# A transformer block with self and cross attention on one core: wider transfers, later weight splits, and another order at the seam to the feed-forward part

## What is computed

```
h = layernorm(x, ln1);  x = attention(h, h) + x          # 16 heads of 64
h = layernorm(x, ln2);  x = attention(h, context) + x
h = layernorm(x, ln3);  a, gate = split(h @ ff_w1 + ff_b1)   # 2 x 1024
x = (a * gelu(gate)) @ ff_w2 + ff_b2 + x
```

## Time and profile before

| | |
|---|---|
| median of 3 runs | 1717.55 us (1717.55 to 1719.23) |
| the profiled execution | 1720.14 us, its span 1718.3 us |
| PE busy | 1702.5 us (99%) |
| VectorE, ScalarE, GpSimd busy | 85%, 69%, 63% |
| moved by DMA | 263.99 MB, mean 154 GB/s |
| mean granted clock of PE | 0.999 |

### The profile page before, as it was taken

How to read it: one execution, slowest core, us unless ns; L and a number is a source line. 1 busy time by engine, 2 the same in 40 slices (tenths; PEclk the granted TensorE clock), 3 DMA queues, 4 the chain that set the end, 5 groups by cost and what they waited for, 6 DMA issues and landing times.

```text
span 1718.3 us, 42977 instructions
## 1 busy us (share of the span) xinstructions
PE 1702.5 (99%) x13628; PEld 1663.1 (97%) x13628; DVE 1467.4 (85%) x3184; ACT 1186.3 (69%) x3245; POOL 1087.9 (63%) x1812
## 2 busy tenths in 40 slices
PE   8999999999999999999999999999999999999999
PEld 8999999999999999999999999999999998888888
DVE  7888988888888888889999999999999997666665
ACT  6777777777777777777778878777777775222222
POOL 6777777766666666687778877777777665122211
PEclk9999999999999999999999999999999999999999
DMA  7777777676656666677777787776666662212110
GB/s 208 186 184 179 185 183 178 171 179 164 155 152 153 153 154 167 158 172 186 186 188 192 193 192 179 184 180 168 167 167 168 163 172 55 74 50 64 66 44 25
DMA packets 286641, 263.99 MB, mean 154 GB/s; under 512 B 102225, under 2 KB 246737, under 8 KB 286417
## 3 DMA queue, kind: packets, MB, share of 16 engines
q1 hardware_dynamic: 232624, 248.12, 57.1%
q10 hardware_dynamic: 53792, 13.12, 3.7%
HBM read 70.40 MB, written 24.90 MB: 55 GB/s over the span
## 4 chain that ended last, share of the span: by engine, by line
PE 90%; DVE 2%; SPq 2%; DMA 2%; POOL 2%; issue 1%; ACT 1%; ACTq 0%; POOLq 0%; DVEq 0%
PE QKB L341 19%; PE PVB L400 13%; PE PTB L355 12%; PE WOP L380 10%; PE VB L316 9%; PE S L303 6%; PE S L302 6%; PE PTB L920 5%; PE S L920 5%; PE QKB L936 3%; PE VB L936 3%; DMA RX<-QKS 1%; SPq L433 1%; SPq L435 1%; ACT PT L507 0%
## 5 line engine op out<-in xcount | busy, mean ns | idle before, releaser
L507 ACT ACTIVATE PT<-S,NM 128x256 f32<-128x256 f32 x1024 | 472.1, 474 | 186.0 <-DVE NM L613 185.6
L595 DVE TENSOR_TENSOR PL<-PTB,PH 128x512 fp32r<-128x512 f32 x512 | 349.4, 683 | 81.5 <-ACT PH L526 77.4
L811 POOL TENSOR_TENSOR ON<-ON,RB 128x256 f32<-128x256 f32 x256 | 188.9, 738 | 278.4 <-DVE ON L633 264.7
L613 DVE TENSOR_REDUCE NM<-S 128x2 f32<-128x512 f32 x512 | 325.9, 677 | 0.0
L526 ACT ACTIVATE PH<-PTB 128x1024 fp32r<-128x1024 f32 x256 | 263.4, 1029 | 90.3 <-PE PTB L355 87.3
L355 PE MATMUL PTB<-IDN,PT 128*128 128x128 f32 x2048 | 266.1, 273 | 0.1
L302 PE MATMUL S<-RX 128*128 128x256 f32 x1012 | 253.9, 283 | 0.2
L303 PE MATMUL S<-RX 128*128 128x256 f32 x1012 | 253.7, 283 | 0.0
L355 PEld LDWEIGHTS PTB<-IDN,PT 128*128 128x128 f32 x2048 | 229.5, 140 | 1.2 <-DVE PL L595 1.1
L380 PE MATMUL WOP<-WO,OT 128*128 128x256 f32 x1536 | 226.3, 283 | 2.3 <-POOL OT L816 2.3
L633 DVE TENSOR_TENSOR ON<-PVB,ON 64x256 f32<-64x256 f32 x512 | 213.1, 416 | 3.5
(11 more groups left out here) (142 smaller groups left out, 3142.4 us busy)
## 6 DMA issues: line engine op xcount, KB each, us to landing
RX<-QKS SPq DMA_DIRECT2D x506, 192.0 KB, 2.9
RX<-QKS SPq DMA_DIRECT2D x506, 128.0 KB, 2.8
RB<-denominators SPq DMA_DIRECT2D x512, 64.0 KB, 2.6
out_dram<-XR SPq DMA_DIRECT2D x32, 256.0 KB, 2.8
rows<-XN SPq DMA_DIRECT2D x24, 256.0 KB, 2.5
rows<-HF SPq DMA_DIRECT2D x23, 256.0 KB, 2.3
XR<-in_x_dram SPq DMA_DIRECT2D x16, 256.0 KB, 3.1
denominators<-RDT SPq DMA_DIRECT2D x256, 16.0 KB
```

Source lines behind the costliest of these rows:

```text
L507: last = e.activation(PT[:, c % 2, j * S:(j + 1) * S], S1[:, i, qt * S:(qt + 1) * S], ACT.Exp, bias=NM[:, j:j + 1], accum_out=DEN[:, c % 2 ...
L595: e.tensor_tensor(PL[:, cols], PTB[:, i, :], PH[:, s % 2, cols].bitcast(F32), ALU.subtract).then_inc(a.dve_pl, 1)
L613: e.tensor_reduce(NM[:, i * TT:(i + 1) * TT], S1[:, i, :].rearrange("p (t s) -> p t s", t=TT), AX.X, ALU.max, negate=True).then_inc(a.dve_ ...
```

## The change

1. `spread_den`: one transfer to all 128 partitions in place of two to 64 each. The source has the dimensions 2 (heads), 64 (the same row again, step 0) and 256. The counts on d_rb fall from 32 to 16 for each spread.
2. `stage`, `stage_rows`: one transfer for a staged matrix in place of two, except for the last 64 rows of the matrices with 192 rows; `staged(load)` gives the new counts.
3. `pool_weights`: the second halves of both output matrices are split one slot later (c = 5 to 8 and 131 to 134).
4. Chunk 0 is normalised in four slots, from ATT - 12 on, one tile of 256 columns each; the store of its second half moves from ATT - 9 to ATT - 8.
5. At slot ATT ScalarE does a Gelu on one column ahead of its first real one, after a wait for the transposes of slot ATT - 2; the first real Gelu waits for these too, not for the last ones, and the second waits for the small one (s_tab).
6. GpSimd makes RSTD of chunk 1 before its slot ATT + 2, not after that slot and the bias additions of chunk 0.
7. VectorE does unit 3 before its slot ATT + 3 (the last residual addition of attention).

The core of the diff:

```diff
@@ act_slot
             if c == ATT:
+                e.wait_ge(a.pe_t, ATT - 1)
+                e.activation(FG[:, 1, 0:1], B1[:, PAIRS:PAIRS + 1], ACT.Gelu).then_inc(s_tab, 1)
                 act_ffn(e, Slot(0, FU, 2))
@@ pool_split_wo, pool_split_w
+        def staged(load):
+            return 16 * (load + sum(load >= n for n in (2 + 3, 2 + 5)))
-                e.wait_ge(d_wst, 32 * load)
+                e.wait_ge(d_wst, staged(load))
@@ pool_weights
-            if HALF <= c < PAIRS:
-                pool_split_wo(e, 0, 1, c)
+            if HALF < c <= PAIRS:
+                pool_split_wo(e, 0, 1, c - 1)
...
-            if SLOTS + 1 < c <= SLOTS + 1 + HALF:
-                pool_split_wo(e, 1, 3 + NCH, HALF + c - SLOTS - 2)
+            if SLOTS + 2 < c <= SLOTS + 2 + HALF:
+                pool_split_wo(e, 1, 3 + NCH, HALF + c - SLOTS - 3)
@@ pool_slot, save_den
-                e.wait_ge(d_rb[s % 2], 32 * (s // 2 + 1))
+                e.wait_ge(d_rb[s % 2], 16 * (s // 2 + 1))
@@ act_ffn
                 if c == 0:
-                    e.wait_ge(a.pe_t, ATT)
+                    e.wait_ge(a.pe_t, ATT - 1)
+                if c == 1:
+                    e.wait_ge(s_tab, 1)
@@ dve_attention_slot
-            if c == ATT - 11:
+            if c == ATT - 12:
                 e.wait_ge(a.s_ht, 4 * B)
                 e.wait_ge(a.pl_ct, 2 * B)
-                dve_normalize(e, zero_ffn, fs, 0, ROWS, (0, 1))
-            if c == ATT - 10:
-                dve_normalize(e, zero_ffn, fs, 0, ROWS, (2, 3))
+            if ATT - 12 <= c < ATT - 8:
+                dve_normalize(e, zero_ffn, fs, 0, ROWS, (c - ATT + 12,))
@@ sync: stage, stage_rows, spread_den, the loop
-            def stage(src, dst=STG[:, :]):
-                h = P // 2
-                for part, rows in ((slice(0, h), src[0]), (slice(h, P), src[1])):
-                    e.dma_start(dst[part], rows).then_inc(d_wst, 16)
+            def stage(rows, part=slice(0, P)):
+                e.dma_start(STG[part, :], rows).then_inc(d_wst, 16)
...
-                for i in range(2):
-                    e.dma_start(RB[OWN[i], s % 2, :],
-                                DS[s % 4, TT * i:TT * (i + 1), :].rearrange("t p -> (t p)").partition_broadcast(P // 2)) \
-                        .then_inc(d_rb[s % 2], 16)
+                e.dma_start(RB[:, s % 2, :], DS[s % 4, 0:2 * TT, :].rearrange("(i t) p -> i (t p)", i=2).unsqueeze(1)
+                            .to_broadcast([2, P // 2, S])).then_inc(d_rb[s % 2], 16)
...
-                if c in (ATT - 10, ATT - 9):
-                    store_ffn_rows(0, c - ATT + 10)
+                if c in (ATT - 10, ATT - 8):
+                    store_ffn_rows(0, (c - ATT + 10) // 2)
@@ gpsimd
-            run_slots(0, ATT + 3, ATT, lambda sl: pool_attention_slot(e, sl))
+            run_slots(0, ATT + 2, ATT, lambda sl: pool_attention_slot(e, sl))
+            e.wait_ge(fs.dve_xn, 2)
+            pool_rstd(e, zero_ffn, fs, 1)
+            pool_slot(e, Slot(ATT + 2, ATT))
@@ vector
-            for j in range(3):
+            for j in range(2):
                 dve_slot(e, Slot(ATT + 1 + j, ATT))
-                if j < 2:
-                    dve_ffn(e, Slot(1 + j, FU, 2))
+                dve_ffn(e, Slot(1 + j, FU, 2))
+            dve_ffn(e, Slot(3, FU, 2))
+            dve_slot(e, Slot(ATT + 3, ATT))
             e.wait_ge(a.dve_xo, 2 * B)
-            ffn(e, dve_ffn, 3)
+            ffn(e, dve_ffn, 4)
```

More of the change, by code:

```diff
@@ L174, in block_kernel @@
         d_wst = sem("d_wst")
+        s_tab = sem("s_tab")
         d_wo = [sem(f"d_wo{n}") for n in range(2)]
@@ L1191, in _ @@
             load_wo(e)
-            def stage(src, dst=STG[:, :]):
-                h = P // 2
-                for part, rows in ((slice(0, h), src[0]), (slice(h, P), src[1])):
-                    e.dma_start(dst[part], rows).then_inc(d_wst, 16)
+            def stage(rows, part=slice(0, P)):
+                e.dma_start(STG[part, :], rows).then_inc(d_wst, 16)
             def stage_rows(w):
-                v = w.rearrange("(g p) n -> p g n", p=P)
-                stage((v[0:P // 2], v[P // 2:P]), STG[:, :].rearrange("p (g n) -> p g n", n=D))
+                e.dma_start(STG[:, :].rearrange("p (g n) -> p g n", n=D),
+                            w.rearrange("(g p) n -> p g n", p=P)).then_inc(d_wst, 16)
             def store_rows(n):
@@ L1224, in save_den @@
                 if s >= 4:
-                    e.wait_ge(d_rb[s % 2], 32 * ((s - 4) // 2 + 1))
+                    e.wait_ge(d_rb[s % 2], 16 * ((s - 4) // 2 + 1))
                 e.dma_start(DS[s % 4, :, :].rearrange("j (b r) -> b j r", b=4),
@@ L1235, in spread_den @@
                     e.wait_ge(s_ow, s + 1)
-                for i in range(2):
-                    e.dma_start(RB[OWN[i], s % 2, :],
-                                DS[s % 4, TT * i:TT * (i + 1), :].rearrange("t p -> (t p)").partition_broadcast(P // 2)) \
-                        .then_inc(d_rb[s % 2], 16)
+                e.dma_start(RB[:, s % 2, :], DS[s % 4, 0:2 * TT, :].rearrange("(i t) p -> i (t p)", i=2).unsqueeze(1)
+                            .to_broadcast([2, P // 2, S])).then_inc(d_rb[s % 2], 16)
             def stage_cross(n):
                 w, k = (ca_wq, ca_wk, ca_wv)[n // 2], n % 2
[L1244 to L1247, removed]
-                else:
-                    stage((w[P:DC, :], w[P:DC, :]))
+                if n % 2 == 0 or n == 1:
+                    stage(w[k * P:(k + 1) * P, :])
+                else:
+                    stage(w[P:DC, :], slice(0, P // 2))
+                    stage(w[P:DC, :], slice(P // 2, P))
             def stage_ffn(n):
@@ L1254, in stage_ffn @@
                     w = ff_w1[n // 2 * P:(n // 2 + 1) * P, n % 2 * CH:(n % 2 + 1) * CH]
-                    stage((w[0:P // 2, :], w[P // 2:P, :]))
+                    stage(w)
                 else:
@@ L1366, in _ @@
             for chunk in range(1, NCK):
-                pool_rstd(e, zero_ffn, fs, chunk)
+                if chunk > 1:
+                    pool_rstd(e, zero_ffn, fs, chunk)
                 pool_ffn_split(e, chunk)
```

## The result

The changed kernel takes 1979.71 us, the kernel before 1718.18 us beside it: ratio 1.1514, 95% interval [1.1498, 1.153]. It is some 260 us slower. I had forecast slower as the likeliest sign, but 1828 us, and the range ended at 1960 us.

What follows compares the result with a forecast made beforehand. TensorE, busy 1702.5 of 1718.3 us, was taken as the bound, with DMA a near second. From 1717.5 us, 9 us of gains off and 120 us for the spread on gave 1828 us; 8-in-10 range 1706 to 1960 us.

Steps and rivals of the forecast that it cites:

- the mechanism: Spread of denominators, every slot: outermost size 2 confines the single transfer to two DMA engines; slower, 1730 to 2000 us, chance 0.60.
- Rival B: Spread of denominators: all sixteen engines take it, or two keep up; only the gains stay, 1708 us; chance 0.28.
- the gains: All edits but the spread: splits 2.3, normalisation 1.2, seam 4.2, staging 1, about 9 us (bounds 1 and 11).
- seam: Between attention and feed-forward: early Gelu table 0.5, TensorE's wait 2.2, half clock 1.5; gain 4.2 us (bounds 0.5 and 4.5).
- splits: Output projections in both attentions: splitting one slot later removes TensorE's two waits for OT; gain 2.3 us (bounds 0 and 2.3).
- normalisation: Chunk 0 before feed-forward: one tile in each of four slots stops two slots stretching; gain 1.2 us (bounds 0 and 1.3).
- staging: SyncE's queue: one issue fewer per staged matrix, about 20 times, so RX copies land earlier; gain 1 us (bounds 0 and 3).
- the 120 us for the spread on two engines: Attention slots: excess from two confined engines, taken a third of the way up between 22 and 359 us.
- The bounds: Spread's excess over attention slots: 22 us if two engines run at best speed, 359 us if contended speed stays.
- The 50 ns for a packet of 1 KB: Spread's packet time, read at 302.3 us; 56 more packets on each of two engines cost 2.8 us per slot.
- The statements on the profile: Whole kernel, if two engines: TensorE about 93%, RX waits nearly every slot, RX landing 4 us or more, spread's about 5.
- Rival C: Attention slots: two engines keep contended speed, TensorE falls to half clock at times; 2067 us or more; chance 0.08.

Runs made afterwards that it cites:

- experiment 4: Changed kernel with the one-transfer spread at outermost size 4 instead of 2, same packets and bytes, partitions 32 to 127 get wrong rows: 1726.44 us.
- experiment 5: Changed kernel with the one-transfer spread at outermost size 16, reciprocals written eight times over so the rows are right: 1709.28 us.
- experiment 9: Kernel before with one gain at a time: seam edits alone (early Gelu table, RSTD, unit 3) 1713.85 us; later splits alone 1716.12; four-slot normalisation alone 1717.24.
- experiment 3: Changed kernel with SyncE issuing the spread last in its slot, behind the store of denominators and the RX copies: 1839.79 us.
- experiment 6: Changed kernel with the spread filling only partitions 0 to 63 from the third slot on (32 packets per engine, denominators partly wrong): 1718.08 us.
- experiment 8: Changed kernel with the spread issued last in its slot and, from the third slot on, filling only partitions 0 to 63: 1715.38 us.
- experiment 1: Changed kernel with the old spread (two transfers to 64 partitions each), all else as changed: 1708.6 us, ratio 0.9949 to the kernel before.

## Why the prediction was right in direction and wrong in size

**Right: the mechanism.** The one-transfer spread runs on two engines. The share of 0.13 to 0.15 and the count of packets in flight show it, and sizes 4 and 16 (experiments 4 and 5) show that the outermost size decides and not the single transfer. Rival B falls: neither do all sixteen engines take it, nor do two keep up. The rule of the Trainium skill (DMA: Bandwidth & Descriptors, "Rules for kernel authors": an outermost dimension below 16 confines the transfer to at most that many engines) agrees with all three sizes measured. Its advice to replace two transfers on partition halves by one of 128 partitions holds at size 16, with no gain, and costs 271 us at size 2.

**Right: the gains.** Forecast 9 us, measured 8.8 with the old spread. By parts: seam 4.2 against 3.6, splits 2.3 against 2.7, normalisation 1.2 against 1.7; staging, taken as 1, gave a difference of 1.0 that is within the noise. One sentence on the staging fails: GpSimd's wait for STG in the first output matrix did not go in the changed kernel, it is 1.81 us at 44.81 us. At the seam the signs came as forecast: the table load starts at 1436.53 us in experiment 9 (about 1438 forecast), and in the changed kernel VectorE's wait of 5.29 us is gone and the granted clock is 1.00 from 1700 to 1740 us.

**Wrong: one term of the sum, the 120 us for the spread on two engines, which measured 271.** The bounds held, 22 and 359 us; 271 lies three quarters of the way up, not a third. The step that failed is the sentence that took a third of the way "since the lag itself removes the contention". It counts work, bytes and packets per engine and slot, as if the two engines always had work waiting. In the changed order they are behind another limit too: the store of the denominators is issued right behind a spread and waits for it in the same two engines, SyncE waits for the store before the next spread, and four RX copies wait behind SyncE, so that the next work for all engines is issued late. The spread to the store's landing had become a loop, and 58% of the chain. I had named the wait for a late resource (RX), but had not gone through what SyncE itself waits for: in the kernel before it is ON of GpSimd, 132.6 us, and the store's 3.1 us gave no warning.

A second number was misread. The 50 ns for a packet of 1 KB is the mean of a stretch in which 31 of 179 packets are of 4 B; those of 1 KB alone took 58 ns. With 58 ns the upper bound would have been some 110 us higher (56 x 8 ns x 251 slots), and the 271 would lie near the middle of the bounds.

Experiments 3, 6 and 8 separate the two. Excess over the 1708.6 us of experiment 1:

```
                         64 packets   48 packets   32 packets
spread ahead of store      271 us       79.5 us      9.5 us
spread last in the slot    131 us         -          6.8 us
```

With the other order the same 64 packets cost 131 us; the remaining 140 us go with the order. That 131 is near the 120 forecast is luck: the prediction had RX late, and in experiment 3 it is RB that is late (433.0 us of GpSimd's waits, 61.2 us of ScalarE's for RX). The late order has no run at 48 packets. If a packet too many costs 48 ns there too, its 131 us are 11 packets, that is a kink at 53 instead of 41 packets; the two orders would then differ in how much fits into a slot and not in the price. This is an estimate, not tested. That the order costs by leaving the two engines without work is argued, not shown: from 300 to 800 us no packet is in flight for 0.6% of the time and exactly one for 3.7%, against 0.0 and 0.2% in experiment 3; 4.3% of the whole span would be 85 us, less than the 140. The rest may be in how long the RX copies of each order take under contention (3.4 and 4.2 us, against 3.3 and 3.8 in experiment 3). This stays open.

**The statements on the profile.** TensorE's share of 93%: right. Waits for RX at the QKS copy in nearly every slot: 222 of 254, right. Landing of the RX copies from 2.8 us to 4 or more: 4.2 for those of 128 KB, but 3.4 for those of 192 KB, half right. Landing of the spread about 5 us: the page gives none. DMA share hardly changed: wrong, 0.57 to 0.61 for 0.62 to 0.77; the bytes are the same and the span is longer. Slots lengthen most where the share was 0.77: right, 6.9 and 6.8 us against 6.5 and 6.4.

**Rival C** priced no relief at 2067 us and had the clock fall. The clock did fall (0.50, that is 1.2 GHz, from 353 to 356 us, above, after TensorE had waited 1.97 us for RX until 352.56 us; 0.97 to 0.99 over the stretches) without the contended speed holding throughout. A mean of 0.99 is 1% of the span or some 20 us at most. Of the 261 us more, 130 are booked as busy TensorE (1832.6 for 1702.5). The ends of matmuls are modelled, and three groups that grew (S, QKB, PTB) account for only 41 of them; I take this division as rough.

## What to carry to other kernels

Before two broadcasts are merged into one transfer, look at the outermost size of the merged pattern: 2 and 4 moved the same bytes through two and four engines here, and the mean DMA share does not show it (it fell, from 0.76 to 0.59 in the first stretch), while a share of 2/16 in a slice of 1 us does. Then follow the small transfers that are issued behind the confined one and ask who waits for them: if the issuing queue itself does, the cost can be twice that of another order (271 against 131 us). The cost has a kink: it is little (9.5 us at 32 packets) while the confined engines fit into the period, and between 48 and 64 packets each cost its full time in every period, so price it from the point where they are full.

## What the hardware showed that I had not expected

Half of a 16 KB store went out within 2 us and the other half 5 to 6 us later: this transfer was as late as the fullest of its engines. Two engines working alone moved 41 to 48 GB/s, about the 21.2 B per ns each that all sixteen reached at 339 GB/s. And between 48 and 64 packets the cost in the whole kernel was 48 ns a packet, near the 46 ns that a packet of 1 KB took while two engines worked alone, although other transfers shared the engines.
